# Splitting the first pair's weights a stage earlier in a float32 chain of attention layers

## The reference

```python
h = _layer_norm(x, ln1_scale, ln1_offset)
x = res + _cross_attention(h, xf_1, wq1, bq1, wk1, bk1, wv1, bv1, wo1, bo1, bias_k1, bias_v1)
res = x
h = _layer_norm(x, ln2_scale, ln2_offset)
x = res + _cross_attention(h, xf_2, wq2, bq2, wk2, bk2, ...)
# inside _cross_attention
qh = (q_in @ wq + bq).reshape(b, q_len, H, K)
kh = (kv_in @ wk + bk).reshape(b, t, H, K)
vh = (kv_in @ wv + bv).reshape(b, t, H, K)
logits = jnp.einsum('bqhk,bthk->bhqt', qh, kh) / scale
weights = jax.nn.softmax(logits, axis=-1)
```

## Time and profile before

| | |
|---|---|
| median of three runs | 1069.89 us (1069.20 to 1071.33) |
| the profiled execution | 1071.58 us, its span 1069.8 us |
| PE, DVE, ACT, POOL busy | 89%, 73%, 57%, 29% of the span |
| mean granted clock of TensorE | 0.944 of full speed |
| stage L0m | about 169.9 to 210.7 us |
| stage L1a, head until the first scores | 211.5 to 236.07 us |

### The profile page before, as it was taken

One profiled execution on the slowest core, in us unless ns is written; L12 is line 12 of the kernel. 1 busy time (PEld: TensorE's weight loads), 2 busy tenths in 40 slices (PEclk: granted clock), 3 DMA queues, 4 the chain that ended last, 5 costly groups with the idle time before them and its releaser, 6 DMA issues. The chain is left out here.

```text
span 1069.8 us, 17955 instructions
## 1 busy us (share of the span) xinstructions
PE 950.5 (89%) x6616; PEld 807.2 (75%) x6616; DVE 777.5 (73%) x1621; ACT 606.4 (57%) x1375; POOL 312.2 (29%) x321
## 2 busy tenths in 40 slices
PE   5888886899999999999899999999587898779958
PEld 5766665788999999998789989898576666656647
DVE  3486775468878888886688988878664788568864
ACT  3597873236565555554365555556534787267842
POOL 3354540050221222221121232200004555445510
PEclk8899997989999999999899999999888799889989
DMA  5995005140110111110210111000106820394020
GB/s 174 257 238 81 2 1 215 41 160 1 41 40 1 40 41 40 41 40 2 79 41 1 41 40 40 1 1 2 67 18 159 208 46 2 106 243 64 1 85 21
DMA packets 39506, 72.71 MB, mean 68 GB/s; under 512 B 6550, under 2 KB 23960, under 8 KB 37244
## 3 DMA queue, kind: packets, MB, share of 16 engines
q1 hardware_dynamic: 39420, 71.56, 24.9%
HBM read 55.28 MB, written 16.27 MB: 67 GB/s over the span
## 5 line engine op out<-in xcount | busy, mean ns | idle before, releaser
L1383 ACT CAST L1a_probsT_hi<-L1a_bank 128x512 fp32r<-128x512 f32 x128 | 69.0, 589 | 86.4 <-PE L1a_bank L1259 86.3
L1207 POOL TENSOR_SCALAR L1a_wo_hi<-L1a_stage 128x512 fp32r<-128x512 f32 x16 | 10.4, 649 | 349.1 <-PE L1a_sums L74 340.8
L1418 ACT ACTIVATE L1a_probs<-L1a_scores,L1a_neg_max 128x512 f32<-128x512 f32 x128 | 86.9, 684 | 33.4 <-DVE L1a_bias_shifted L1543 28.9
L1539 DVE TENSOR_REDUCE L1a_top<-L1a_scores 128x2 f32<-128x1024 f32 x64 | 78.2, 1222 | 18.6 <-PE L1a_scores L74 18.6
L1454 DVE TENSOR_TENSOR L1a_probsT_lo<-L1a_bank,L1a_probsT_hi 128x512 fp32r<-128x512 f32 x128 | 82.1, 682 | 0.2
L72 PE MATMUL L1a_bank<-L1a_probsT_hi,L1a_v_hi 128*128 128x256 f32 x256 | 73.7, 288 | 9.4 <-DVE L1a_probsT_lo L1454 9.4
L1385 ACT ACTIVATE L1a_attended_hi<-L1a_bank,L1a_cols 128x256 fp32r<-128x256 f32 x64 | 30.5, 477 | 84.0 <-PE L1a_bank L74 83.7
L72 PE MATMUL L1a_bank<-L1a_w_hi,ctxT_hi 128*128 128x256 f32 x256 | 74.8, 292 | 0.0
L444 POOL TENSOR_SCALAR L0a_probs<-L0a_probs,L0a_inverse 128x768 f32<-128x768 f32 x64 | 57.2, 906 | 58.2 <-DVE L0a_inverse L713 58.2
L73 PE MATMUL L1a_bank<-L1a_probsT_lo,L1a_v_hi 128*128 128x256 f32 x256 | 73.0, 285 | 0.0
L74 PE MATMUL L1a_bank<-L1a_probsT_hi,L1a_v_lo 128*128 128x256 f32 x256 | 72.9, 285 | 0.0
(11 more groups left out here) (424 smaller groups left out, 3098.5 us busy)
## 6 DMA issues: line engine op xcount, KB each, us to landing
L1a_stage<-in_L_w SPq DMA_DIRECT2D x15, 1024.0 KB, 4.7
L0m_fold_wq<-in_L_wqT SPq DMA_DIRECT2D x2, 2048.0 KB, 12.7
L0a_k_dram<-L0a_kT_hi SPq DMA_DIRECT2D x8, 384.0 KB, 10.1
L0a_k_stack<-L0a_k_dram SPq DMA_DIRECT2D x4, 576.0 KB
L0a_w_qkv<-L0a_k_dram SPq DMA_DIRECT2D x4, 576.0 KB
L0a_wide_wo<-in_L_wo SPq DMA_DIRECT2D x1, 2048.0 KB, 16.6
L0a_wide_wo<-in_L_wo SPq DMA_DIRECT2D x2, 1024.0 KB, 17.7
L0m_stage<-in_L_wm SPq DMA_DIRECT2D x4, 512.0 KB, 6.4
```

Of the source, the lines that this page charges most:

```text
L1383: nc.scalar.copy(out, source).then_inc(ring.hi_done, 1)
L1418: nc.scalar.activation(probs[:, g % 2, qt, :], scores[:, qt, :], ACT.Exp, bias=neg_max[:, g % 2, qt:qt + 1], accum_out=row_sum[:, g % 2, q ...
L1539: link(nc.vector.tensor_reduce(top[:, :], scores[:, :, :], AX.X, ALU.max))
```

## The change

A class `FirstPair` holds the stage buffer and the split weights of the first pair outside of the stages. Its load is issued by SP in stage L0m behind `fold_wq`, and POOL scales and splits it there, behind its root of the norm. In the wide layers the four chunked loads, three ACT and three DVE operations on weights and their semaphores are gone. Both layers now begin in the same order: six projections, the transposes, two projections, and so on. In layer one PE waits only for `split_done` first. DVE's column work moves behind all eight key and value splits, and DVE and ACT wait for the small loads (`small_loaded`, all of them) before the first key.

```diff
+class FirstPair:
+    def load(self, sp):
+        sp.dma_start(self.stage[:, :], self.source).then_inc(self.loaded, 16)
+
+    def split(self, nc, pool):
+        pool.wait_ge(self.loaded, 16)
+        link = Chain(pool, self.step)
+        link(nc.gpsimd.tensor_scalar(self.stage[:, 0:512], self.stage[:, 0:512], float(DW) ** -0.5, 1.0, ALU.mult, ALU.mult))
+        link(nc.gpsimd.tensor_scalar(self.w[0][:, :], self.stage[:, 0:1536], 1.0, 1.0, ALU.mult, ALU.mult))
+        nc.gpsimd.tensor_tensor(self.w[1][:, :], self.stage[:, 0:1536], raw(self.w[0][:, :]), ALU.subtract).then_inc(self.split_done, 1)
...
                 fold.load(sp, io)
+                cfg["first_pair"].load(sp)
...
             parts.root(nc, pool)
+            if fold:
+                cfg["first_pair"].split(nc, pool)
...
-            for c in FIRST_ORDER:
-                sp.dma_start(stage[0][:, c * 512:(c + 1) * 512],
-                             io["L1_w1"][0][:, c * 512:(c + 1) * 512]).then_inc(first_loaded[c], 16)
...
                 if layer:
                     pe.wait_ge(w_ready, PAIRS + 1)
                 else:
-                    parts[layer].transpose(nc, pe, ring, keep)
+                    pe.wait_ge(first_pair.split_done, 1)
                 for n, item in enumerate(KV):
-                    if n in (0, 4) and layer == 0:
-                        pe.wait_ge(first_lo, 1 if n == 0 else 2)
                     project(PAIRS + 1 if layer else 0, item)
-                    if n == NORM_AT - 1 and layer:
+                    if n == NORM_AT - 1:
                         parts[layer].transpose(nc, pe, ring, keep)
...
-            for c in FIRST_ORDER[:3]:
-                act.wait_ge(first_loaded[c], 16)
-                nc.scalar.mul(w[0][0][:, c * 512:(c + 1) * 512], stage[0][:, c * 512:(c + 1) * 512],
-                              1.0 if c else scale).then_inc(first_hi, 1)
...
                 parts[layer].statistics(nc, link, keep["x"], 1e-5, True)
-                if layer:
-                    for item in KV[:2]:
-                        low(job_of[p0 + 1, item], destination(p0 + 1, item), bias_of(p0 + 1, item))
+                if layer == 0:
+                    dve.wait_ge(small_loaded, 48 * LAYERS)
+                p = p0 + 1 if layer else 0
+                for item in KV[:2]:
+                    low(job_of[p, item], destination(p, item), bias_of(p, item))
                 parts[layer].apply(nc, dve, keep["x"], True)
+                for n, item in enumerate(KV[2:], 2):
+                    low(job_of[p, item], destination(p, item), bias_of(p, item))
+                    if n == NORM_AT - 1:
+                        split_norm(layer)
```

More of the change, by code:

```diff
@@ L215, in _, with __init__ @@
                                         raw(to[0][:, kt, t0 * P:t0 * P + 512]), ALU.subtract).then_inc(ring.freed_by(job), 1)
+class FirstPair:
+    def __init__(self, nc, mem, io):
+        self.source = io["L1_w1"][0]
+        self.stage = mem.enter_context(nc.sbuf_tensor("first_stage", [P, 2048], F32))
+        self.w = [mem.enter_context(nc.sbuf_tensor(f"first_w_{part}", [P, 1536], F32R)) for part in ("hi", "lo")]
+        self.loaded, self.step, self.split_done = (nc.alloc_semaphore(f"first_{what}") for what in ("loaded", "step", "split"))
+    def load(self, sp):
[6 more added lines that the diff above has]
+        nc.gpsimd.tensor_tensor(self.w[1][:, :], self.stage[:, 0:1536], raw(self.w[0][:, :]), ALU.subtract).then_inc(self.split_done, 1)
 def narrow_attention(nc, io, keep, cfg):
@@ L1025, in turn, with wide_attentions @@
         return last
-def wide_attentions(nc, io, keep, audT):
+def wide_attentions(nc, io, keep, audT, first_pair):
     name = "L1a"
@@ L1060, in wide_attentions @@
     with Phase(nc, name) as ph:
-        stage = [ph.sb(f"stage{j}", [P, 2048]) for j in range(2)]
-        w = [ph.hilo(f"w{j}", [P, 1536]) for j in range(2)]
+        stage = [first_pair.stage, ph.sb("stage1", [P, 2048])]
+        w = [first_pair.w, ph.hilo("w1", [P, 1536])]
         wo = [ph.hilo(f"wo{j}", [P, 2, D]) for j in range(2)]
@@ L1144, in wide_attentions @@
         sums_full, sums_free = ph.sem("sums_full"), ph.sem("sums_free")
[L1145 to L1146 removed]
+        ones_set = ph.sem("ones_set")
         block = ph.block()
[L1148 removed]
         def unit(g):
@@ L1307, in queries @@
                 ring.wait_evacuated(pe, job_of["norm1", layer])
-                if layer == 0:
-                    pe.wait_ge(first_lo, 3)
                 project(p, QS[0])
@@ L1520, in _ @@
                     dve.wait_ge(ones_set, 2)
-                for n, item in enumerate(KV):
-                    p = p0 + 1 if layer else 0
-                    if n >= 2 or not layer:
-                        low(job_of[p, item], destination(p, item), bias_of(p, item))
-                    if n == NORM_AT - 1 and layer:
-                        split_norm(layer)
                 dve.wait_ge(cols_scaled, LAYERS)
```

63 lines of the change are left out of this document (23 added, 40 removed).

## The result

The changed kernel takes 1073.19 us (median of ten runs, 1068.62 to 1074.63) against 1069.59 us for the kernel before (ten runs, 1064.18 to 1072.12). The ratio is 1.0035, with a 95% interval from 1.0019 to 1.0051: 3.7 us slower, between 2.0 and 5.5. The profiled execution took 1072.18 us, its span 1070.4.

What follows compares the result with a forecast made beforehand. PE, busy 89% of the span, was taken as the bound, with time only in its gaps and low clock. Stage ahead 0, mark +0.6 and clock +1.7 gave +2.3 us on 1069.89: 1072.2, range 1067.5 to 1074.5.

Steps and rivals of the forecast that it cites:

- clock: PE's pause before the first unit's transposes brings the low clock: 1.7 us taken, bounds 0 to 3.4.
- mark: PE's first projection behind the first unit's transposes, 246.01 us before: forecast 246.35 to 246.85, 0.6 us late.
- Stage ahead: Stage L0m: weights there near 193, POOL's splits done by 200.4; cost 0 to 0.9 us, 0 taken.
- The start of PE and its key projections: Layer one's head: PE starts with the other engines at 211.5; four key projections of 1.4 us run until 217.1.
- The small loads: Layer one's head: ACT and DVE wait for them before evacuating keys; landing 217.6 to 219.3, 218.9 taken.
- T: Layer one's head: norm evacuated by DVE's serial line at 218.9 + 0.75 + 8.68 = 228.3; 1.0 earlier or 0.5 later.
- Behind T: Layer one's head: columns ready at T + 2.9, POOL's second-pair weights T + 7.9 to 8.3, first scores end T + 8.3.
- The hold: First unit's normalisation: POOL's 3.5 us operation holds DVE's L1552; L1554 starts at 244.1 to 244.6, against 243.76 before.
- three: Layer one's head late as forecast, first pause also costs the clock, plus 0.9 us in stage ahead: 5.4 us, 1075.3; chance 0.12.
- Rival one: First unit: DVE's short operations reach the port before POOL's long one, not held; 2.7 us gained, 1067.2; chance 0.20.

Runs made afterwards that it cites:

- early-loads kernel: The changed kernel with columns, key biases and output biases loaded in the stage ahead, behind the first pair's weights: 1065.45 us, ratio 0.9969.
- PE kept busy: The changed kernel with 16 extra matmuls ahead of the first value projection and 5 ahead of the bias scores, results overwritten: 1068.49 us, ratio 1.0003.
- the kernel with the columns early: The changed kernel with DVE's small column work moved between the first and second value split: 1072.75 us, ratio 1.0038.
- the runs with POOL's waits: The changed kernel with POOL's third-pair work waiting, in both layers, for the first unit's normalised probabilities: 1074.11 us; for the second unit's: 1072.07 us.
- the split ahead alone: The kernel before with the first pair's weights split in the stage ahead, layer one keeping its old order: 1069.38 us, ratio 1.0021.
- the kernel before with POOL's wait: The kernel before with POOL's third-pair work waiting, in both layers, for the first unit's normalised probabilities: 1071.75 us, ratio 1.0032.

## Why the prediction was right

The forecast was 1072.2 us, slower, by a lost clock and a later mark; 1073.19 was measured, a median inside the range from 1067.5 to 1074.5. The sum (+2.3) fits head one (+2.5), but its parts are divided otherwise than I wrote, and that they add up to the same is luck.

- **Stage ahead, 0.** Right. The weights were there at 193.0 ("more likely near 193"), POOL ended at 199.1 with 200.4 as the bound. The last splits were held, as the rule of the Trainium skill (SBUF — State Buffer, section SBUF: two separate sides) says and no row of before showed; they had the slack.
- **The start of PE and its key projections.** Right: they ran from +0.0 to +5.7.
- **The small loads.** Late by 0.7: ACT was released at +8.15, my value was +7.4 and my range ended at +7.8. The last of them landed 4.9 us behind its issue, or a little less. The early-loads kernel shows that this wait, which I carried as a start time only, decides between the change winning and losing.
- **T**, the norm's last split. The step that failed. Predicted at +16.8 (at most +17.3), measured +18.8. Of the 2.0 us, 0.7 are the loads. The rest is DVE's line, 9.8 us from the first key split to the norm's last instead of 8.68, and ACT's start. It is PE at the low clock: DVE waited 0.38 and 1.80 us for the first two value projections, each at half speed, and with PE kept busy T is at +17.0. I had named this and given it 0.5 us; it costs 1.9.
- **Behind T** (counted from POOL's first row behind it, at 228.13). The columns were ready at T + 2.8 (2.9), POOL's second pair at T + 7.8 (7.9 to 8.3). The first scores ended at T + 10.2, not T + 8.3, since the second query and the scores fell into the second low stretch. The sum had no term for this stretch: I judged a pause by its length, 1.63 us harmless and 3.00 us not, and here a pause of 1.25 us with the 16-column matmuls behind it was followed by 3.4 us at 0.50.
- **The hold.** Right in kind and size of effect: POOL's long operation began at T + 12.1 (12.2 to 12.6 forecast) and DVE reached L1554 of before (L1544 here) 0.34 us behind its end. But L1540 was held, since DVE came to this work at T + 13.8 and not T + 11.9, by the low clock. In the same way PE's pause before the transposes was 0.82 and 0.49 us, not 2.4 to 2.7.
- **The mark and the clock.** The mark is +37.0 behind the stage's start where I had +34.9 to +35.4; behind it the clock stayed at 1.00 where I had charged 1.7 us. The mark is 1.7 to 2.2 us later than I had it, about what I charged for the clock behind it. That term, half of 3.4 us because the pause lay between two others, was a guess and did not come; what came is T's lateness of 2.0 us, 0.7 of it the loads and the rest mostly the clock ahead of the mark. POOL's operation, which starts from T, passed it on to the mark, and it covered the second low stretch: without that stretch, in the kernel with the columns early, it ends at +34.6 as it does at +34.4 here, and holds another operation until then. Of the rivals, three comes nearest in mechanism (the first pause costs the clock too), without its 3.4 us behind the mark and its 0.9 in the stage ahead. Rival one, no hold, is out: L1540 is long and ends with POOL. But the runs with POOL's waits also show that the hold is worth less than I thought of it: taken off the first two units it gives 1.5 us of head one, 0.7 of which is an earlier T in that execution (+18.15), whose first low stretch lasted 3.4 us and not 6.8.
- **Head two**, 0.8 longer, had no term in the sum. Its code is not changed, and it varies by more than that in kernels with no edit there (25.1 to 26.5 us). The longer hold of L1531 makes it here, and the passage ahead of it is 1.8 us shorter without the low stretch. I had written that a shift at the mark reaches the end undiminished; in this profile it did not: at layer two's fifth maximum, 1.5 us are left. What remains up to the 3.7 us of the time is not explained; one profile cannot show the median of ten runs.
- Open is why the split ahead alone is slower than its heads say, by 2.9 us (1.3 outside its interval).

## What to carry to other kernels

When a wait is taken away, list what the next one in the same place waits for, the small transfers above all: here six small loads, the last a broadcast of 128 KB, hidden before behind the weights, decided whether 4 us were won or 2.5 lost in the head. Issuing them a stage earlier cost nothing that shows: that stage took 40.0 to 41.3 us in the five kernels that do it and 40.4 to 41.9 in the others. A pause of the TensorE had a second price behind it when the clock fell, and it was paid by whoever waited for PE then. Starting POOL's operation of 3.5 us later did not cure its hold by itself; look first at what it will meet there, and compare stages from their own start, not by absolute times.

## What the runs showed of the hardware

- A DVE operation that reads SBUF alone and begins behind POOL's long one lasted to its very end, however small: 0.16 us became 3.32 when it started 0.15 us behind (241.70 against 241.55). A value split, which reads PSUM, kept its 0.69 us at 226.31 beside POOL's 3.53 us from 225.23 (the kernel before with POOL's wait). The Trainium skill (the same page and section) states the lock for operations with two SBUF inputs or in a two-port mode; L1542 has two such inputs, and the trace agrees. A cast with one took 0.74 instead of 0.43 us beside POOL at 193.16; that fits the second kind, though no trace shows the mode it ran in.
- POOL's own row grows where DVE was there first: its low part took 3.81 us at 195.31, with DVE's split running until 195.77, and 3.43 to 3.53 us in the wide layers.
- PE's clock can fall with PE hardly idle: the second low stretch, 234.5 to 237.9, came behind a pause of 1.25 us and 2.7 us of 16-column matmuls, and came again in the kernel that filled that pause (233 to 236.6). In the four kernels with the columns early, where the same matmuls follow without a pause, it did not come at that place. What decides it is not shown.
